# One scan for the eight decay triangles of a step

## The reference

```python
def step(S, inp):
    qt, kt, vt, gt, bt = inp
    S = S * jnp.exp(gt)[..., None, None]
    mem = jnp.einsum('bhk,bhkv->bhv', kt, S)
    delta = (vt - mem) * bt[..., None]
    S = S + jnp.einsum('bhk,bhv->bhkv', kt, delta)
    o = jnp.einsum('bhk,bhkv->bhv', qt * scale, S)
    return (S, o)
```

## Time and profile before

| | |
|---|---|
| median of 3 runs | 3080.88 us (3077.23 to 3086.05) |
| span of the profiled execution | 3086.7 us |
| PE, PEld busy | 2650.6 us (86%), 2187.0 us (71%) |
| DVE busy | 2285.6 us (74%) |
| ACT, POOL busy | 1761.1 us (57%), 591.9 us (19%) |
| line 739, scans 128x128, 512 of them | 223.3 us busy, mean 498 ns |
| line 716, masks 128x512, 768 of them | 523.2 us busy, mean 681 ns |
| recurrence (turns) | about 135 to 2660 us of the span |

### The profile page before, as it was taken

One profiled execution on the slowest core, in us unless ns is written; L12 is line 12 of the kernel. 1 busy time (PEld: TensorE's weight loads), 2 busy tenths in 40 slices (PEclk: granted clock), 3 DMA queues, 4 the chain that ended last, 5 costly groups with the idle time before them and its releaser, 6 DMA issues. The chain is left out here.

```text
span 3086.7 us, 71844 instructions
## 1 busy us (share of the span) xinstructions
PE 2650.6 (86%) x22496; PEld 2187.0 (71%) x22496; DVE 2285.6 (74%) x5647; ACT 1761.1 (57%) x4019; POOL 591.9 (19%) x733
## 2 busy tenths in 40 slices
PE   1389899999898898898898898898898899587887
PEld 0268778788787787787787787787787787354455
DVE  4479888798797797888888797798897798133434
ACT  1157666676676676676676676676676677211121
POOL 0022222222222222222222122222222222000000
PEclk6699999999999999999999999999999999798888
DMA  2301020001000100010001000100010000200000
GB/s 83 97 25 38 2 65 19 21 14 53 26 25 14 53 25 26 14 53 26 26 14 53 26 25 14 53 25 26 14 53 26 26 14 1 83 1 28 27 27 7
DMA packets 93598, 96.20 MB, mean 31 GB/s; under 512 B 31217, under 2 KB 82106, under 8 KB 93250
## 3 DMA queue, kind: packets, MB, share of 16 engines
q1 hardware_dynamic: 93250, 91.44, 9.8%
HBM read 72.10 MB, written 2.54 MB: 24 GB/s over the span
## 5 line engine op out<-in xcount | busy, mean ns | idle before, releaser
L716 DVE TENSOR_TENSOR dr_w<-dr_ps,mask 128x512 bf16<-128x512 f32 x768 | 523.2, 681 | 170.5 <-PE dr_ps L526 167.6
L730 DVE SCALAR_TENSOR_TENSOR dr_y<-dr_ps,dr_cw,dr_y 128x255 f32<-128x255 f32 (+2 forms) x1344 | 574.6, 475 | 29.1 <-ACT dr_y L855 22.5
L848 ACT CAST dr_tt<-dr_ps 128x512 bf16<-128x512 f32 x768 | 460.4, 600 | 1.2 <-PE dr_ps L546 1.2
L845 ACT CAST dr_tn<-dr_ps 128x512 bf16<-128x512 f32 x640 | 374.9, 586 | 147.6 <-PE dr_ps L539 147.6
L630 PE MATMUL dr_ps<-dr_w,dr_am 128*128 128x96 f32 x3072 | 421.9, 281 | 2.5 <-ACT dr_w L907 2.5
L630 PEld LDWEIGHTS dr_ps<-dr_w,dr_am 128*128 128x128 f32 x3072 | 382.8, 194 | 11.0 <-ACT dr_w L907 3.0
L546 PE MATMUL dr_ps<-dr_tt,dr_w 128*128 128x128 bf16 x3072 | 297.7, 219 | 74.6 <-DVE dr_w L716 74.6
L552 PE MATMUL dr_ps<-dr_hb,dr_wqk 128*128 128x256 f32 x1024 | 287.7, 430 | 23.7 <-DMA dr_hb<-hT 22.7
L526 PE MATMUL dr_ps<-dr_tn,dr_b 128*128 128x128 bf16 x3072 | 297.1, 219 | 0.0
L539 PEld LDWEIGHTS dr_ps<-dr_w,dr_tt 128*128 128x128 bf16 x2560 | 186.4, 98 | 141.5 <-issue 70.4
L907 ACT COPY dr_w<-dr_ps 128x384 f32<-128x384 f32 x384 | 188.8, 492 | 134.2 <-PE dr_ps L630 134.0
(11 more groups left out here) (187 smaller groups left out, 4843.6 us busy)
## 6 DMA issues: line engine op xcount, KB each, us to landing
dr_abc<-scr_a SPq DMA_DIRECT2D x64, 512.0 KB, 3.9
dr_hb<-hT SPq DMA_DIRECT2D x64, 256.0 KB, 2.5
dr_bcb<-scr_b SPq DMA_DIRECT2D x128, 64.0 KB, 3.2
ex_modb<-scr_mod SPq DMA_DIRECT2D x4, 1024.0 KB, 6.7
dr_wo<-in_Wo SPq DMA_DIRECT2D x1, 3072.0 KB, 11.3
dr_wv<-in_Wv SPq DMA_DIRECT2D x8, 384.0 KB, 4.0
dr_wg<-in_Wg SPq DMA_DIRECT2D x8, 384.0 KB, 3.9
p_x<-in_x SPq DMA_DIRECT2D x4, 512.0 KB, 6.2
```

The source lines that it names most:

```text
L716: v.tensor_tensor((tn if l == 0 else w16)[:, us, :], ps[:, (X0, X1)[g], :].rearrange("p (u n) -> p u n", u=QH), bc(mask[:, l, :], 1, QH), ...
L730: v.scalar_tensor_tensor(y[:, slot, x:T], ps[:, (A0, A1)[n % 2], off:off + T - x], cw[:, t, TAPS - 1 - x:TAPS - x], y[:, slot, x:T], ALU.m ...
L845: act.copy(tn[:, us, :], ps[:, (X2, X1)[g], :].rearrange("p (u n) -> p u n", u=QH)).then_inc(s["tn_ok"], 1)
L848: act.copy(dst, ps[:, (X0, X2)[g], :].rearrange("p (u n) -> p u n", u=QH)).then_inc(s["tt_ok"], 1)
```

## The change

A step's eight triangles are made by one scan over 4 x 256 = 1024 elements. A second copy of the identity, `id8`, repeats it eight times side by side. So that a chunk doesn't take over the last product of the one before, the first decay of each chunk is set to zero in `tmp["a"]`, after the running products of line 325 have read it; SyncE's store of the decays waits for that (`az_ok`). `dec` is now laid out as head, chunk, token, `decays` stands in slot 2 alone, and `dec_ok` counts one a step.

```diff
@@ prepare, SyncE
-            sp.wait_ge(a_ok, 1)
+            sp.wait_ge(az_ok, 1)
@@ prepare, VectorE, behind the scans of line 325
+            v.wait_ge(bcum_ok, 2 * CH)
+            v.memset(t["a"][:].rearrange("p (n t) -> p n t", t=P)[:, :, 0:1], 0.0).then_inc(az_ok, 1)
@@ delta_rule
-        dec = sb("dec", [P, U, P])
+        dec = sb("dec", [P, QH, CH, P])
+        id8 = sb("id8", [P, U * P])
@@ tables
-        A_AT = {0: [("qk", 0)], 1: [("taps", 0, 0)], 2: [("taps", 0, 1), ("qk", 1), ("decays", 0)],
+        A_AT = {0: [("qk", 0)], 1: [("taps", 0, 0)], 2: [("taps", 0, 1), ("qk", 1), ("decays",)],
-                11: [("scores", 1), ("decays", 1)], 12: [("decayed", 1, 0), ("values", 0)],
+                11: [("scores", 1)], 12: [("decayed", 1, 0), ("values", 0)],
@@ batch, SyncE
-                    wait_apart(sp, s["dec_ok"], (it - NB + 1) * U, s["passed_sp"])
+                    wait_apart(sp, s["dec_ok"], it - NB + 1, s["passed_sp"])
@@ decays, VectorE
-            def decays(st, c):
+            def decays(st):
                 it, m = st
                 v.wait_ge(s["a_ld"], (it + 1) * 16)
-                for h in range(QH):
-                    u = c * QH + h
-                    v.tensor_tensor_scan(dec[:, u, :], abc[:, m, h, c * P:(c + 1) * P], ident, 0.0,
-                                         ALU.mult, ALU.add).then_inc(s["dec_ok"], 1)
+                v.tensor_tensor_scan(dec[:].rearrange("p h c t -> p (h c t)"),
+                                     abc[:, m].rearrange("p h t -> p (h t)"), id8[:], 0.0,
+                                     ALU.mult, ALU.add).then_inc(s["dec_ok"], 1)
@@ keys, decayed, VectorE
-                v.tensor_tensor(cj[:], gam[:, m, 0:QH], dec[:, 0:QH, P - 1], ALU.mult).then_inc(s["cj_ok"], 1)
+                v.tensor_tensor(cj[:], gam[:, m, 0:QH], dec[:, :, 0, P - 1], ALU.mult).then_inc(s["cj_ok"], 1)
-                        gam[:, m, u:u + 1], bc(dec[:, u, :], 1, 2), ALU.mult, ALU.mult)
+                        gam[:, m, u:u + 1], bc(dec[:, 2 * a + side, c, :], 1, 2), ALU.mult, ALU.mult)
@@ set-up of delta_rule, VectorE, ahead of its memsets
+            v.tensor_copy(id8[:].rearrange("p (u t) -> p u t", u=U), bc(ident, 1, U)).then_inc(s["set_ok"], 1)
-            v.wait_ge(s["set_ok"], 6)
+            v.wait_ge(s["set_ok"], 7)
```

More of the change, by code:

```diff
@@ L136, in prepare @@
             sem(n) for n in ("var_ok", "rstd_ok", "h0_ok", "ss_ok", "ms_ok", "rr_ok", "hn_ok", "tr_ps", "ht_ok"))
-        z_ps, absz_ok, u_ok, sp_ok, a_ok, eb_ok, beta_ok, bt_ps, bcum_ok = (
-            sem(n) for n in ("z_ps", "absz_ok", "u_ok", "sp_ok", "a_ok", "eb_ok", "beta_ok", "bt_ps", "bcum_ok"))
+        z_ps, absz_ok, u_ok, sp_ok, a_ok, az_ok, eb_ok, beta_ok, bt_ps, bcum_ok = (
+            sem(n) for n in ("z_ps", "absz_ok", "u_ok", "sp_ok", "a_ok", "az_ok", "eb_ok", "beta_ok", "bt_ps", "bcum_ok"))
         acts, done, late, passed, passed_pool = (sem(n) for n in ("acts", "done", "late", "passed", "passed_pool"))
@@ L461, in _ @@
             sp.dma_start(gw[:], A["gnorm_w"]).then_inc(s["c_ld"], 16)
-            sp.wait_ge(s["set_ok"], 6)
+            sp.wait_ge(s["set_ok"], 7)
             def weights(q):
@@ L758, in keys @@
                 v.wait_ge(s["gam_ok"], it + 1)
-                v.wait_ge(s["dec_ok"], it * U + QH)
-                v.tensor_tensor(cj[:], gam[:, m, 0:QH], dec[:, 0:QH, P - 1], ALU.mult).then_inc(s["cj_ok"], 1)
+                v.wait_ge(s["dec_ok"], it + 1)
+                v.tensor_tensor(cj[:], gam[:, m, 0:QH], dec[:, :, 0, P - 1], ALU.mult).then_inc(s["cj_ok"], 1)
                 v.wait_ge(s["cj_ok"], it + 1)
@@ L767, in decayed @@
                 it, m = st
-                v.wait_ge(s["dec_ok"], it * U + QH * (c + 1))
+                v.wait_ge(s["dec_ok"], it + 1)
                 v.wait_ge(s["kk_ps"], it * CH + c + 1)
@@ L978, in _ @@
             pool.memset(vo[:], 1.0).then_inc(s["set_ok"], 1)
-            pool.wait_ge(s["set_ok"], 6)
+            pool.wait_ge(s["set_ok"], 7)
             run(pool, on)
```

## The result

The changed kernel takes 3100.1 us (median of 3098.5 to 3106.3), against 3083.5 us for the kernel before beside it: ratio 1.0057, 95% interval 1.0040 to 1.0075. It is slower by about 18 us; 3105.5 was forecast, with 3089 to 3122 around it. The profiled execution has a span of 3104.4 us, 17.7 more than before.

The account below looks back on a forecast made before the run. TensorE was taken as the bound, with VectorE just in time in slot 2. Terms +58.0 - 21.4 - 13.8 + 1.8 = +24.6 us on 3080.9 gave 3105.5 us, range 3089 to 3122.

Parts of the forecast that it names:

- Part 1: One scan of 1024 takes 2.19 us to the next start; VectorE's work falls by 1.15 us a step, 74 us in all.
- the 60 to 70 named as a sign: Over the whole kernel, VectorE's busy time was to fall by some 60 to 70 us.
- Part 2: Slot 2: the mask comes 0.92 us later and TensorE waits that long ahead of L539 in 63 turns, +58.0 us.
- Part 3: Slot 11 loses its scans, so the gap ahead of L546 shrinks: 0.35 us in 61 turns, -21.4 us.
- Part 4: Loads of next inputs start about 9 us earlier, shortening twelve loop jumps by 1.15 us each, -13.8 us.
- Part 5: Preparation: stores of the decays come ahead of the b stores, +1.8 us; the id8 copy costs 0.
- the jumps give nothing back: Loop jumps: their extra time comes from the code fetch's phase, not the loads; 3119 us, chance 0.15.
- The steep slope: Slot 2: the long scan takes 2.54 us; +46.6 us in sum, 3127 us, chance 0.07.
- the cheap scan: Slot 2: the long scan takes 1.25 us, so no stall; 3047.5 us, chance 0.05.
- VectorE is the true bound: Whole recurrence: the 74 us of VectorE work saved come off whole; 3007 us, chance 0.03.
- The partial cover: Slot 2: the stall is 44 us, or the mask's delay is taken back somewhere unseen; 3081 to 3092 us, chance 0.10.

Follow-up runs that it names:

- the pair in slot 9: The kernel before with its second four scans moved from slot 11 to slot 9, without and with one more SyncE wait delaying loads: ratios 0.9894 and 0.9926.

## Why the prediction was right, step by step

The span grew by 17.7 us. By the starts of the scans and the last matmuls it divides so: +2.1 up to the first scan, +3.5 in the first three turns, +20.0 in 41 plain turns, -10.9 in 19 turns with a jump, +2.7 from the last scan to the end of the recurrence, +0.3 behind it. Forecast was +24.6. The two large terms that were off were off the same way, the stall by 6 us and the jumps by 6, and 4 to 5 us that weren't forecast, at the start and the end of the recurrence, took part of it back; that the total is off by 7 only is in part luck.

**Part 1, the scan's length: right.** 2.19 us to the next start, as taken; 2.28 us with its tail. From 128 to 1024 elements the duration grows from 0.40 to 2.28 us, 2.10 ns an element, twice the plain product's 1.04. The measured rate agrees with the half throughput of the Trainium skill ("DVE: opcode table, instruction layouts, handler registers and perf-mode slots", section "Datapath and trigger behaviour"). By the starts VectorE's work fell by 1.15 us a step, as forecast; its busy time fell by 61 us, within the 60 to 70 named as a sign.

**Part 2, the stall: right in place, 0.1 us too large.** The mask came 0.92 us later, and the matmul of L542 stands 2.91 us behind the scan's start where L539 stood 2.09: 0.82 us. I had taken the slack from the weight load, which was next to nothing, and the load's start did move by 0.92. But the load ran beside the last matmul of L695: the load began 0.10 us ahead of its own matmul, which started no sooner than 0.22 us after L695's last, the distance at which those follow each other too. So the matmul had 0.1 us in hand. Over 63 turns that is 6 us less than forecast.

**Part 3, slot 11: right.** 0.36 us for 0.35; the last full turn of the kernel before had been the model of it. For the same reason that turn had nothing left to gain, so 60 turns gained it and not 61. A plain turn: 0.82 - 0.36 = 0.46, and 36.23 - 35.77 = 0.46 was measured.

**Part 4, the loads: right, and too small.** 4.62 to 3.38 us in the twelve jumps is 1.24 for 1.15. The 19 turns with a jump gained 10.9 us in spite of 19 x 0.46 = 8.8 us of stall: 19.7 us and not 13.8. The gaps of all 19 jumps give 82.5 - 67.9 = 14.6 of it, and a second gap that stands at each jump, ahead of L630 (L633 now), 44.0 - 42.2 = 1.8. The sum had no term for the clock behind a jump, which was at 1.2 GHz for 31 us less; what that gave isn't measured by itself. It isn't shown to be the loads' doing either: late loads brought back 10 us of slow clock in the changed kernel, but the pair in slot 9 has 180 us of it both with the wait and without. By the run with late loads and the pair in slot 9, loads are worth 9 to 24 us in the medians, so 13.8 is within what was measured and no run fixes the size better.

**Part 5, once only: right for what was named.** The b stores are issued at 112.12 us instead of 109.70, with the phase ahead of them 0.45 us late in this execution, so 2.0 for 1.8. The copy for id8 took 0.69 us, beside SyncE's issues of L463 and L464 (until 121.3 us), and nothing waited for it.

```profile
110.28 1.79 SPq L166 DMA_DIRECT2D scr_a<-p_t_a  x4
...
112.12 1.86 SPq L170 DMA_DIRECT2D scr_b<-p_t_bc  x4
...
115.57 0.69 DVE L831 COPY dr_id<-const 128x1024 f32<-128x1024 f32 x1 [4.53 <-PEq L104]
```

Not forecast were +3.5 us in the first three turns, of which 2 or less were in the sum by parts 2 and 3 (the first turn grew by 0.7, the second by 0.5, the third by 2.4). In the third TensorE's stall ahead of L542 was 2.0 us, for 1.07 before, and the granted clock fell behind it. The windows of that turn after and, in the last row, before:

```profile
210.00:215.00 5.00, 3.59 (x24) 3.09 (x25) 4.75 (x10) 2.17 (x5) 1.04 (x1) 0.78 0.01 3
...
215.00:220.00 5.00, 5.00 (x53) 4.50 (x52) 3.34 (x8) 4.18 (x10) 0.61 (x1) 0.88 0.00 0
```

```profile
210.00:215.00 5.00, 5.00 (x59) 4.78 (x57) 4.73 (x13) 4.69 (x11) 0.61 (x1) 1.00 0.00 0
```

It goes with the long slot 2: the third turn also has 38.0 us with the loads late and 38.8 with eight scans in slot 2, with such a stall and a fall of the clock at 211 us, while the kernel before and the five others have 35.3 to 36.1 us and no fall there. The first turns weren't tried by themselves; nor were the 2.7 us at the end, where 0.8 is the last step's stall, with no relief against it, as slot 11 had little to give there. The rest of those 2.7 stays open.

**The rivals.** That the jumps give nothing back is out by the late loads (4.40 against 3.38 us). The steep slope and the cheap scan are out by 2.19 us. That VectorE is the true bound is out twice: 61 us less of VectorE's work went with 18 us more time, and in slots 2 and 9 the merged kernel is no faster than the unmerged one. The Trainium skill ("Perfetto Trace Analysis", section "Optimizing Scalar/DVE Operations") says that larger operations help if the engine is saturated. No run here shows a saturated VectorE (71% to 74% busy), so the rule wasn't tried; this engine had a deadline to meet, not too much to do. The partial cover was the case to a small part, the 0.1 us that the matmul had in hand.

## What to carry to other kernels

Where two in-order engines hand work to each other, cost an edit at the next handover behind each place that it touches: work that grows ahead of a tight one is paid in full, work that shrinks is worth only as much as the next release allows, and here moving four small instructions to idle time gained 33 us, while merging eight into one at a tight handover lost 18. Follow every wait between the new place and the next free time, not just the one that was tight before: the gate matmuls' wait for the taps cost two experiments their forecast. And ask what a buffer that comes free earlier will start, since loads that no one waited for made the loop's jumps shorter.

## What the runs showed of the hardware

A transfer issued 1.6 to 2.5 us before TensorE's gap at a loop jump makes the gap longer: 3.1 to 3.8 us without one and 3.7 to 5.6 with one, over all kernels run here and without the jumps beside a reload of weights. In the gap one packet of 16 KB runs on the instruction queue, and beside the transfer it starts later or runs longer. That it is the transfers' place and not TensorE's code was tried twice, by one added wait on a queue that computes nothing.

A wait of TensorE costs 0.16 to 0.20 us more than its gap between modelled matmuls shows, since a matmul is drawn longer (0.38 or 0.21 us) than the time after which the next one can start (0.22 or 0.04). In an account of turns, go by starts, or subtract the gaps and see if the rest is the same.

A scan and a GpSimd operation that reads SBUF exclude each other, in whichever order they come: 0.37 us on the scan's side, 0.40 us on the square's.
